# Bias copied one column at a time, and the last inner tile padded to 128 rows

## The reference, cut to what matters

```python
xn = layernorm(x)                              # x: 1024 x 256
qkv = xn @ qkv_w + qkv_b                       # 16 heads of 128
scores = q @ k.T + alibi_mask                  # causal, one slope per head
ctx = softmax(scores) @ v
attn = ctx @ out_w + out_b
h = silu(xn @ lut[gate_idx].T) * (xn @ lut[up_idx].T)   # 688 inner columns
ffn = h @ lut[down_idx].T
return x + attn + ffn
```

## Time and profile before

| what | value |
|---|---|
| median of 3 runs (lowest, highest) | 553.34 us (552.51, 555.99) |
| span of the profiled execution | 551.5 us |
| mean granted clock of TensorE | 0.996 |
| PE busy | 522.4 us, 95% of the span |
| DVE busy | 436.5 us, 79% |
| POOL busy | 337.6 us, 61% |
| ACT busy | 304.1 us, 55% |

### The profile page before, as it was taken

How to read it: one execution, slowest core, us unless ns; L and a number is a source line. 1 busy time by engine, 2 the same in 40 slices (tenths; PEclk the granted TensorE clock), 3 DMA queues, 4 the chain that set the end, 5 groups by cost and what they waited for, 6 DMA issues and landing times. The chain is left out here.

```text
span 551.5 us, 10612 instructions
## 1 busy us (share of the span) xinstructions
PE 522.4 (95%) x3216; PEld 466.0 (85%) x3216; DVE 436.5 (79%) x1051; ACT 304.1 (55%) x653; POOL 337.6 (61%) x391
## 2 busy tenths in 40 slices
PE   7897999999999999999999999999999899989998
PEld 6686879888898889887988889888988799878887
DVE  6799897889778887989788987888798969754541
ACT  3556665556564746566555656474656547654420
POOL 3565867568566956586756856695658647872100
PEclk8999999999999999999999999999999999999999
DMA  7200100001000100010000100010000000000001
GB/s 272 93 20 1 39 20 20 2 23 35 0 19 19 38 0 19 0 38 19 19 0 23 34 0 19 19 38 0 19 0 0 19 2 2 1 1 1 1 23 54
DMA packets 7429, 13.14 MB, mean 24 GB/s; under 512 B 1008, under 2 KB 3184, under 8 KB 7280
## 3 DMA queue, kind: packets, MB, share of 16 engines
q1 hardware_dynamic: 7408, 12.88, 7.4%
HBM read 11.83 MB, written 1.05 MB: 23 GB/s over the span
## 5 line engine op out<-in xcount | busy, mean ns | idle before, releaser
L1025 POOL TENSOR_TENSOR w_ffn<-w_ffn,term 128x1088 f32<-128x1088 f32 x60 | 152.0, 2534 | 0.0
L658 ACT ACTIVATE work<-work,neg_max 128x128 f32<-128x128 f32 (+7 forms) x128 | 98.7, 771 | 42.8 <-DVE neg_max L843 42.8
L665 ACT ACTIVATE p_t_hi<-ps_t 128x512 fp32r<-128x512 f32 (+1 forms) x192 | 86.0, 483 | 47.4 <-DVE bias_now L808 27.7
L876 DVE TENSOR_TENSOR p_t_lo<-ps_t,p_t_hi 128x512 fp32r<-128x512 f32 (+1 forms) x192 | 98.7, 542 | 6.6 <-ACT p_t_hi L665 6.5
L999 POOL TENSOR_TENSOR pad<-entry 128x1 f32<-128x1 f32 x128 | 25.8, 201 | 124.9 <-DVE inv_sum L870 124.3
L1000 POOL TENSOR_SCALAR work<-work,inv_sum 128x128 f32<-128x128 f32 (+7 forms) x128 | 101.8, 795 | 0.0
L843 DVE CUSTOM_DVE_ANT_0 work<-ps_s,alibi 128x128 f32<-128x128 f32 (+7 forms) x128 | 96.1, 751 | 5.4 <-issue 5.4
L511 PE MATMUL ps_t<-ident,work 128*128 128x128 f32 x576 | 84.6, 273 | 8.5 <-DVE p_t_lo L876 6.3
L511 PEld LDWEIGHTS ps_t<-ident,work 128*128 128x128 f32 x576 | 68.5, 140 | 17.2 <-DVE p_t_lo L876 4.0
L392 PE MATMUL ps_u<-p_t_hi,v_hi 128*128 128x512 f32 x192 | 69.4, 361 | 0.0
L392 PE MATMUL ps_s<-qk_hi 128*128 128x256 f32 (+2 forms) x192 | 67.3, 350 | 1.3 <-DVE neg_max L843 1.3
(11 more groups left out here) (121 smaller groups left out, 1196.8 us busy)
## 6 DMA issues: line engine op xcount, KB each, us to landing
qk_raw<-w_qk SPq DMA_DIRECT2D x16, 256.0 KB, 2.6
w_ffn<-idx SPq DMA_DIRECT2D x1, 2176.0 KB, 10.8
v_raw<-w_v SPq DMA_DIRECT2D x8, 256.0 KB, 2.5
o_raw<-w_o SPq DMA_DIRECT2D x8, 256.0 KB, 2.6
out<-acc SPq DMA_DIRECT2D x8, 128.0 KB, 1.7
acc<-x SPq DMA_DIRECT2D x2, 256.0 KB, 2.9
acc<-x SPq DMA_DIRECT2D x1, 512.0 KB, 5.8
term<-b_out SPq DMA_DIRECT2D x1, 128.0 KB, 6.1
```

Source lines behind the costliest of these rows:

```text
L658: act.activation(slot(i), slot(i), ACT.Exp, bias=neg_max[:, col:col + 1], scale=-1.0, accum_out=row_sum[:, col:col + 1]).then_inc(exp_done, 1)
L665: act.activation(p_rows(0, i, g), ps_t[:, room, 0:len(turned(i, g)) * P].rearrange("p (j q) -> p j q", q=P), ACT.Copy).then_inc(p_hi, 1)
L876: dve.tensor_tensor(p_rows(1, i, g), ps_t[:, room, 0:len(turned(i, g)) * P].rearrange("p (j q) -> p j q", q=P), p_rows(0, i, g).bitcast(F3 ...
L1025: pool.tensor_tensor(piece, piece, term[:, :], ALU.add).then_inc(term_added, 1)
```

## The change

`next_bias` copies its columns one by one, each with an instruction of its own; only the last counts up `bias_ready`. The two-column copy of step 1 so becomes two one-column copies, the one at the start three; the one-column copy of step 5 is the same as before.

`rows_of` gives 64 rows instead of 48 for the last inner tile, so silu, the product and the high and low part write 64 rows. POOL, at the end of its list, sets rows 64 to 127 of the last h tile to zero, in four instructions of 64x512 (high and low, for both token halves), after it has waited for the last unit of the attention part and for its own last low part of the weights. Each down tile waits for them (`h_padded`) and reads 128 rows of h and of the weights in all of its 18 matmuls. The weights of rows 48 to 127 were zero already.

```diff
--- before.py
+++ after.py
@@ -225,6 +225,7 @@
         scores_masked, inv_ready, p_lo = sem("scores_masked"), sem("inv_ready"), sem("p_lo")
         unit_used, term_ready = sem("unit_used"), sem("term_ready")
         h_ready, h_lo_done, out_ready = sem("h_ready"), sem("h_lo_done"), sem("out_ready")
+        h_padded = sem("h_padded")
 
         based = sem("based")
         iota_done, made, normed, term_added = sem("iota_done"), sem("made"), sem("normed"), sem("term_added")
@@ -315,7 +316,7 @@
 
         def rows_of(u):
 
-            return slice(0, P if u % FT < FT - 1 else REST)
+            return slice(0, P if u % FT < FT - 1 else UP_AT)
 
         def h_tile(part, u):
 
@@ -597,12 +598,12 @@
                     pe.wait_ge(out_ready, t - 1)
                 c, q = t // 4, (t % 4) * P
                 pe.wait_ge(h_lo_done, (c + 1) * FT)
+                pe.wait_ge(h_padded, 2 * (c + 1))
                 for f in range(FT):
                     u, at = c * FT + f, DOWN_AT + f * HID
-                    rows = rows_of(u)
                     last = three(ps_t[:, t % 2, 0:HID],
-                                 [h_tile(0, u)[rows, q:q + P], h_tile(1, u)[rows, q:q + P]],
-                                 [ffn_w(0, at, HID)[rows, :], ffn_w(1, at, HID)[rows, :]],
+                                 [h_tile(0, u)[:, q:q + P], h_tile(1, u)[:, q:q + P]],
+                                 [ffn_w(0, at, HID), ffn_w(1, at, HID)],
                                  f == 0, f == FT - 1)
                 last.then_inc(down_done, 1)
 
@@ -805,8 +806,10 @@
             def next_bias(n, p, parity, which):
 
                 at = slice(2 * n + p, 2 * n + p + 1) if isinstance(n, int) else bass.ds(2 * n + p, 1)
-                dve.tensor_copy(bias_now[:, parity, which],
-                                bias[:, at, which].rearrange("p a b -> p (a b)")).then_inc(bias_ready, 1)
+                for one in range(which.start, which.stop):
+                    last = dve.tensor_copy(bias_now[:, parity, one:one + 1],
+                                           bias[:, at, one:one + 1].rearrange("p a b -> p (a b)"))
+                last.then_inc(bias_ready, 1)
 
             def make_alibi(n, p, parity):
 
@@ -925,7 +928,7 @@
                     dve.wait_ge(h_lo_done, u - 1)
                 rows = rows_of(u)
                 up = (ps_s[:, u % 2, HALF:2 * HALF] if u % FT < FT - 1
-                      else ps_s[UP_AT:UP_AT + REST, u % 2, 0:HALF])
+                      else ps_s[UP_AT:2 * UP_AT, u % 2, 0:HALF])
                 dve.tensor_tensor(h_raw(u)[rows, :], up, silu_tile(u)[rows, :], ALU.mult).then_inc(h_ready, 1)
 
             def h_lo_of(u):
@@ -1038,6 +1041,12 @@
             for piece in range(4, PIECES):
                 ffn_lo(piece)
 
+            pool.wait_ge(unit_used, number(PAIRS - 1, LAST, 1, "pv0") + sum(what in ("pv", "out") for what, _ in TAIL))
+            pool.wait_ge(ffn_w_lo, PIECES)
+            for u in (FT - 1, 2 * FT - 1):
+                for part in range(2):
+                    pool.memset(h_tile(part, u)[UP_AT:, :].bitcast(F32), 0.0).then_inc(h_padded, 1)
+
 
 def kernel(**inputs):
     import numpy as np
```

## The result

| | before | after |
|---|---|---|
| median of the runs on one chip | 552.92 us (552.28 to 555.99, 4 runs) | 532.17 us (531.35 to 532.76, 4 runs) |
| ratio, 95% interval | | 0.9616 [0.9589, 0.9644] |
| span of the profiled execution | 551.5 us | 530.9 us |
| middle pair | 59.70 us | 57.16 us |
| down product, first to last start | 19.96 us | 17.15 us |

The changed kernel is 20.8 us faster; 19.7 had been forecast. The profiled execution took 532.76 us, so 1.9 us lie around its span.

The account below looks back on a forecast made before the run. PE was taken to bound the kernel, busy 57.52 of a middle pair's 59.70 us. Copies 16.9 plus padding 2.8 gave 19.7 us off 553.3, so 533.6 us, with an 80% range of 529 to 541.

Parts of the forecast that it names:

- The bound: Middle pairs: PE bounds; its waits of 1.02, 0.18 and 1.33 us go, 2.53 us per pair, 15.2 us in six.
- The held copy: Step 1's two-column DVE copy lasts until POOL's sum ends; split, DVE is past it 1.66 to 1.93 us earlier.
- The second rival: Bias copies: one column is held by POOL like two, so the copies gain nothing; 551.9 us, chance 0.05.
- Half given back: Rival: PE meets later waits for DVE or POOL, half of 16.9 us is returned; 542.1 us, chance 0.13.
- The slower rival: DVE look-ups after the freed copy meet POOL instructions and take up to 1.81 us; 562.7 us, chance 0.02.
- First and last pair: PE's listed idle in these two pairs goes: 1.16 + 0.60 = 1.76 us.
- The padding: Down product: last inner tile at 128 rows removes 0.19 us at each of 15 changes of shape, 2.8 us.
- The terms at nothing: Splitting the other copies, 64 rows in silu to low part, POOL's four memsets, the `h_padded` wait: 0 each.

Follow-up runs that it names:

- experiment with sixteen copies: Changed kernel plus sixteen idle one-column copies ahead of the two bias copies, in each of 15 places: pair 57.74 us, 537.08 us in one run.
- the short sum: Kernel before, two-column copy kept, POOL's sum of step 1 cut from 1088 columns to one: copy 0.15 us, pair 57.15 us, 534.25 us in one run.
- a two-column copy put back: Changed kernel plus one idle two-column copy ahead of the two one-column copies, in each of 15 places: pair 59.94 us, 550.99 us in one run.
- kernels with 64 rows: Changed kernel without memsets, down product reading 64 rows of the last inner tile instead of 128: down product 19.95 us, 535.18 us in one run.
- 8 changes: Copies split, last inner tile at 48 rows, every second token tile taking it first, against 15 changes of shape: down product 18.62 us, 532.89 us in one run.
- look-up late in every pair: Changed kernel with DVE's look-up of step 6 moved to step 7 in every pair: 529.14 us (4 runs), repeated at 529.20 us.
- copies-only profile: Kernel before with only the bias copies split, last inner tile still at 48 rows: 535.52 us (4 runs), ratio 0.967.
- the last experiment: Changed kernel with step 6's look-up moved to step 7 in the last pair alone, 531.51 us; the every-pair version repeated, 529.20 us; executions sorted by granted clock.

## Why the prediction was right

**The bound.** Right: PE bounds the pair, and its starts give the cost. 1.02 + 0.18 + 1.33 = 2.53 us was the term, and 2.54 was measured, 15.2 us in six pairs. Place by place the starts moved by 1.01, 0.25 and 1.32: the small one was costed with a pitch of 0.10 us for the single transpose, and undisturbed it is 0.03. No rival wait took it back. The experiment with sixteen copies is its counterpart: the same two places, the same kind of sum.

**The held copy.** Right, and shown from both sides: the short sum frees a two-column copy (0.15 us), and a two-column copy put back is held again (2.17 us). The second rival, one column held too, is out with the row at 74.92. The Trainium skill's "VectorE: DVE Perf Modes", in "What auto-detection actually checks", gives the two-port mode to one source and a destination in SBUF whose outermost non-unit counts are both even or equal. Two and two were held, and so were three and three, in agreement with it. A copy of one element has no count above one, so the page doesn't promise it the mode, and it wasn't held. "SBUF — State Buffer", in "SBUF: two separate sides", says that a DVE instruction in such a mode and a GpSimd instruction exclude each other for the whole instruction; 2.17 us beside the long sum and 0.15 beside the short one fit. That the copies of two and three columns were held because of a mode is an inference of mine; the runs show only how long they took.

**Half given back.** It didn't come, and no later wait grew into the gap. The one wait listed in the pair after, 0.34 us at 125.34, was 0.34 us before the change too (at 129.55), and the one of 1.75 us in the last pair was 1.75 before (at 485.86). They are what had been left alone.

**The look-ups.** The slower rival didn't come either. Of the eight look-ups in a middle pair one went from 1.44 to 1.67 us (113.83 before, 109.05 after), and together they take DVE 7.95 us instead of 7.72.

**First and last pair.** Here a term was too small. I took PE's idle as it was listed, 1.16 + 0.60 = 1.76 us, although I had just argued that listed idle understates a late start. Before the first middle pair the same transposes came 1.66 us earlier (68.18, where it was 69.84), and in the last pair another 0.89 was won: 2.55 instead of 1.76.

**The padding.** 2.8 us forecast, 2.81 measured. The price per change, 0.19, and that it belongs to the change and not to the rows, is shown by the kernels with 64 rows and with 8 changes.

**The terms at nothing.** The memsets took 0.52 us each (the bound was 0.8) with 11 us to spare. The split of the first three-column copy costs nothing that shows: in both kernels the next copy starts at 24.5. The wait for `h_padded` is not seen: the down product starts right behind the last gate and up matmul.

**The sum.** 15.2 + 1.66 + 0.89 + 2.81 = 20.6 us, the difference of the spans (551.5 - 530.9); 19.7 was forecast, and the 0.8 between is the first and last pair.

## What to carry to other kernels

Look for tiny instructions of DVE with durations of microseconds, and hold them against POOL's timeline: a copy of eight bytes per partition, repeated in every head, cost this kernel 17.9 us, since the instruction behind it frees a bank that PE waits for. Cost a wait of PE by starts (this start less the one before, less the undisturbed pitch), in every place, the first and last turn of the loop too. An instruction moved on DVE is moved against POOL as well: ask which POOL instruction it will now meet.

## What the runs showed of the hardware

- One element per partition isn't held by POOL's sum; two and three are, 2.17 us. Two copies of one column (0.20 us) beat one of two columns there by ten times.
- In a run of matmuls, each change of the number of rows, from 128 to 64 or 48 or back, costs 0.19 us, in two steps of about 0.1 at the first and second matmul of the new shape.
- The start of the run has two lengths. After its first 22 transposes PE waits for DVE, and the granted clock that follows differs. After (2.00 us of wait), in pieces of 2 us; the number behind PE's count is the granted clock:

```profile
8.00:10.00 2.00, 1.93 (x13) 0.72 0.67 266
10.00:12.00 2.00, 2.00 (x11) 0.50 1.03 437
12.00:14.00 2.00, 2.00 (x15) 0.93 0.97 414
```

With the look-up late in every pair (1.59 us of wait):

```profile
8.00:10.00 2.00, 1.96 (x18) 1.00 0.85 321
10.00:12.00 2.00, 1.80 (x16) 1.00 1.01 435
12.00:14.00 2.00, 2.00 (x14) 1.00 0.94 402
```

The clock of 0.50 is the lower level, 1.2 GHz, and 1.00 the higher. In the seven profiles in which the clock fell the wait here had been 1.90 to 2.29 us, once 3.50; in the seven in which it stayed, 1.51 to 1.75. The second copy of the bias, where no spare copies were added, starts at 24.4 or 24.5 with a fall (26.5 in the copies-only profile, the one with 3.50) and at 23.3 or 23.4 without: 1.2 us. The table of the last experiment shows the same step between executions of one kernel. Why the wait differs between executions of one kernel is open; I made no run that changes it.
